# Grouped rows for the top-2 experts of the second block, an earlier softplus, and the scan's B and C rows spread by transfers

## What is computed

```python
# the scan of the first layer: B_t and C_t are 16 numbers per token, the same for all 256 channels
def step(h, t):
    delta_t, B_t, C_t, u_t = t
    dA = jnp.exp(delta_t[..., None] * A)
    h = dA * h + delta_t[..., None] * B_t[:, None, :] * u_t[..., None]
    y = jnp.einsum('bdn,bn->bd', h, C_t)
    return (h, y)
# the expert block of the second layer: E, S, H = 8, 2, 512
logits = jnp.einsum('btd,de->bte', X, Wg) + bg
topv, topi = jax.lax.top_k(logits, S)
w = jax.nn.softmax(topv, axis=-1)
xs = X[:, :, None, :] * w[..., None]
for e in range(E):
    h = jax.nn.silu(jnp.einsum('btsd,dh->btsh', xs, W1[e])) * jnp.einsum('btsd,dh->btsh', xs, W3[e])
    y = jnp.einsum('btsh,hd->btsd', h, W2[e])
    out = out + jnp.where((topi == e)[..., None], y, 0.0).sum(axis=2)
```

## Time and profile before

| | us |
|---|---|
| runs | 2838.62, 2842.82, 2860.75 (median 2842.82) |
| profiled execution, its own time | 2849.43 |
| its span, first to last instruction | 2847.6 |
| PE busy in it | 2609.8 (92%) |
| DVE busy | 1804.3 (63%) |
| ACT busy | 1235.0 (43%) |
| POOL busy | 754.6 (27%) |
| granted TensorE clock, mean | 0.929 of full |
| HBM read, written | 23.56 MB, 2.10 MB |

### The profile page before, as it was taken

The page is one execution under the profiler, slowest core; times in us unless marked ns, Lnnn a source line. Parts: engine busy times, 40 slices in busy tenths (PEclk is TensorE's granted clock), DMA queues, the critical chain, the costliest instruction groups (busy, mean ns, idle before and its releaser), DMA issues.

```text
span 2847.6 us, 35881 instructions
## 1 busy us (share of the span) xinstructions
PE 2609.8 (92%) x10560; PEld 1426.0 (50%) x10560; DVE 1804.3 (63%) x3214; ACT 1235.0 (43%) x2672; POOL 754.6 (27%) x429
## 2 busy tenths in 40 slices
PE   3267999999999999999999999999989999999999
PEld 1033555445554455545555455544555455545654
DVE  3953786567765677657866587557765587644334
ACT  2222563246532464326632466225643266323531
POOL 1311451035400353005510155003630056102200
PEclk8577899999999799998999999899999999998999
DMA  4000000000000000000000000000000000000000
GB/s 165 0 15 8 23 34 19 1 19 31 24 16 1 27 27 20 16 4 30 31 24 1 14 28 27 20 1 27 31 16 16 4 31 31 19 1 26 30 8 4
DMA packets 28590, 61.76 MB, mean 22 GB/s; under 512 B 5464, under 2 KB 5856, under 8 KB 27744
## 3 DMA queue, kind: packets, MB, share of 16 engines
q1 hardware_dynamic: 28384, 59.23, 5.8%
HBM read 23.56 MB, written 2.10 MB: 9 GB/s over the span
## 4 chain that ended last, share of the span: by engine, by line
PE 76%; issue 10%; DVE 8%; ACT 3%; POOL 2%; DMA 0%; SPq 0%; DVEq 0%; POOLq 0%; ACTq 0%
PE G L844 10%; PE G L821 9%; PE G L768 6%; PE G L769 6%; PE G L778 5%; PE G L832 5%; PE FM L821 5%; PE G L812 2%; PE G L861 2%; DVE HS L1250 2%; PE FM L748 2%; PE FM L596 2%; PE G L824 2%; PE G L568 2%; PE FM L812 1%
## 5 line engine op out<-in xcount | busy, mean ns | idle before, releaser
L1032 ACT ACTIVATE HS<-G 128x512 f32<-128x512 f32 x256 | 152.6, 596 | 608.4 <-PE G L769 607.1
L1601 POOL TENSOR_TENSOR Y<-Y,HC 128x1024 f32<-128x1024 f32 x128 | 301.1, 2352 | 351.3 <-DVE HC L1262 351.3
L844 PE MATMUL G<-REG 128*128 128x64 f32 x2560 | 383.4, 283 | 1.8
L1615 POOL TENSOR_TENSOR REG<-REG,cos_t 128x512 f32<-128x512 f32 x128 | 219.8, 1717 | 621.8 <-ACT REG L1051 621.8
L1413 DVE SCALAR_TENSOR_TENSOR HS<-HS,G 128x512 f32<-128x512 f32 x256 | 175.8, 687 | 298.7 <-ACT HS L1032 296.1
L844 PEld LDWEIGHTS G<-REG 128*128 128x128 f32 x2560 | 346.2, 201 | 11.0 <-ACT REG L1071 5.6
L1071 ACT ACTIVATE REG<-G 128x128 f32<-128x128 f32 (+3 forms) x512 | 222.2, 434 | 219.1 <-PE G L832 213.2
L1250 DVE TENSOR_TENSOR_SCAN HS<-DA,D 128x1024 f32<-128x1024 f32 x128 | 312.8, 2444 | 1.3
L821 PE MATMUL G<-REG 64*128 64x256 f32 (+3 forms) x688 | 289.8, 503 | 11.5 <-ACT REG L1063 11.3
L768 PE MATMUL G<-D,up_w 128*128 128x512 f32 x512 | 270.7, 611 | 7.8 <-DVE HC L1420 7.0
L778 PE MATMUL G<-HC,down_w 128*128 128x512 f32 x512 | 265.0, 602 | 3.9 <-DVE HC L1420 3.9
(11 more groups left out here) (249 smaller groups left out, 3947.1 us busy)
## 6 DMA issues: line engine op xcount, KB each, us to landing
REG<-ROT SPq DMA_DIRECT2D x256, 128.0 KB, 2.0
EW<-experts SPq DMA_DIRECT2D x16, 514.5 KB, 4.1
X<-xT SPq DMA_DIRECT2D x8, 256.0 KB, 3.1
W<-weights SPq DMA_DIRECT2D x1, 2048.0 KB, 9.6
up_w<-moe_up SPq DMA_DIRECT2D x1, 2048.0 KB, 15.0
gate_w<-moe_gate SPq DMA_DIRECT2D x1, 2048.0 KB, 19.1
down_w<-moe_down SPq DMA_DIRECT2D x1, 2048.0 KB, 23.4
REG<-xT SPq DMA_DIRECT2D x8, 256.0 KB, 2.6
```

Of the source, the lines that this page charges most:

```text
L844: mm = pe.matmul(G[3][:, col:col + DK], PT[:, n % 2, c * P:(c + 1) * P], V[:, c, j * P + h * DK:j * P + (h + 1) * DK], start=c == 0, stop= ...
L1601: pool.tensor_tensor(Y[:, :, :], Y[:, :, :], HC[:, n % 2, :, :], ALU.add).then_inc(y_add.sem, 1)
L1615: pool.tensor_tensor(ROT, ROT, cos_t[:, :], ALU.mult).then_inc(rope_d.sem, 1)
```

## The change

**Second expert block, by grouped rows.** Tokens are transposed to rows (`XTOK`), multiplied by their first and second pick's weight (`weigh_rows`, two POOL operations), and written to a table in DRAM, `x_rows`, sorted by expert: each expert's rows begin at a multiple of 128, so 15 tiles of 128 rows always suffice (2 x 512 rows, and at most 127 unused ones for each of 8 experts). The place of each row comes from nine bf16 matmuls on counts (`rank`) and a dozen small DVE operations (`places_of`, `number_places`). The scatter is 8 indirect transfers issued by POOL (`scatter`, in attention steps 20 to 33). The tiles come back as `XG`, are transposed on the tensor engine (`turn_rows`, 15 transposes in steps 46 to 52), and each tile is one token use: 8 up and gate matmuls and 4 down matmuls with 128 rows each instead of 512 tokens, one tanh, two DVE operations, one ACT copy, and a store to `y_rows`. The weights of a tile's expert (128 partitions x 6 KB, 786 KB) are loaded for each tile into one of three slots by SP, which reads the expert's number (`load_tile`). In the next attention phase POOL gathers each token's two results by 8 indirect transfers (`gather`, steps 1 to 14) and adds them; four transposes and one DVE add give the output, which is stored then, not at the end of `phase_1`. For the last sequence this stands in `finish`, after everything else.

**B and C by transfers.** `front_b` and `front_c` and the split into bf16 parts are gone. B and C are copied out of PSUM once (`BC`), stored to DRAM (`store_bc`), and for each state a transfer broadcasts B's and C's row to all partitions, 512 KB in SBUF, into one of two slots (`BCS`, `load_bc`). L1245 and L1262 now read their second operand from SBUF, not from PSUM.

**Softplus moved.** Its matmuls, ACT and DVE operations become starts 9, 10 and 11 of `front_start`, behind filter steps 15, 16 and 18 of `phase_1`. POOL's DU, D_skip and XNB copies also move to `phase_1`.

**Smaller.** The semaphores of a norm are merged; `M0` takes the place of `LNI`; the dense weights are no longer loaded at the start; instead `REG` is zeroed by DVE and stored once to `x_rows`, and SP waits for that before it loads the first sequence.

```diff
+MOE_ROWS = P
+MOE_TILES = (S * PICKS + EXPERTS * (MOE_ROWS - 1)) // MOE_ROWS
+SLOTS = 3
+MOE_COLS = 2 * HID + CHUNKS * D
 EXPERT_COLS = HID + CHUNKS * D + CHUNKS + 1
...
+        X_AFTER = {0: 1, 1: 2, 2: 3, 6: 4, 7: 5, 8: 6, 10: 7, 11: 8, 15: 9, 16: 10, 18: 11}
...
+        RANK_AT, PLACE_AT, NUMBER_AT, RETURN_AT = 3, 6, 19, 20
+        GATHER_AT, ADD_AT, WEIGH_AT, SCATTER_AT = (1, 4, 5, 6, 9, 12, 13, 14), 17, 15, (20, 21, 22, 25, 28, 29, 30, 33)
+        STORE_AFTER, ROWS_AFTER = 9, 11
+        TURN_AT = (46, 48, 50, 52)
...
+            def load_rows(b):
+
+                sp.wait_ge(xt_mm.sem, xt_mm.at(b - 1))
+                sp.sem_inc(sp_passed, 1)
+                sp.wait_ge(sc_in.sem, sc_in.at(b))
+                sp.sem_inc(sp_passed, 1)
+                sp.dma_start(XG[:, :, :], x_rows.rearrange("(i r) d -> r i d", r=MOE_ROWS)).then_inc(xg_in.sem, 16)
+
+            def load_tile(t, i):
+
+                k = i % SLOTS
+                if i >= SLOTS:
+
+                    sp.wait_ge(dn_mm.sem, dn_mm.at(t, i - SLOTS + 1))
+                else:
+                    sp.wait_ge(dn_mm.sem, dn_mm.at(t - 1))
+                    sp.sem_inc(sp_passed, 1)
+
+                    sp.wait_ge(place_d.sem, place_d.at(t))
+                sp.sem_inc(sp_passed, 1)
+                e = sp.value_load(tile_i[0:1, i:i + 1], min_val=0, max_val=EXPERTS - 1)
+                sp.dma_start(MW[:, k, :], moe[bass.ds(e, 1), :, :].rearrange("a p c -> (a p) c")).then_inc(mw_in[k].sem, 16)
+
+            def store_tile(t, i):
...
+            def load_bc(b, n):
+
+                if n == 0:
+                    sp.wait_ge(bc_out.sem, bc_out.at(b))
+                    sp.sem_inc(sp_passed, 1)
+                if n >= 2:
+                    sp.wait_ge(hc_mul.sem, hc_mul.at(b, n - 1))
+                else:
+                    sp.wait_ge(hc_mul.sem, hc_mul.at(b - 1))
+                sp.sem_inc(sp_passed, 1)
+                sp.dma_start(BCS[:, n % 2, :, :], bc_rows.rearrange("(k n) s -> n k s", n=STATES)[n].partition_broadcast(P)).then_inc(bc_in[n % 2].sem, 16)
...
+            def up_gate(b, i):
+
+                if i >= 2:
+
+                    pe.wait_ge(hh_d.sem, hh_d.at(b, i - 1))
+                pe.wait_ge(xt_copy.sem, xt_copy.at(b, i // TILES + 1))
+                pe.wait_ge(mw_in[i % SLOTS].sem, mw_in[i % SLOTS].at(b, i // SLOTS + 1))
+                g = 2 * (i % 2)
+                for half in range(2):
+                    for c in range(CHUNKS):
+                        at = half * HID + c * P
+                        mm = pe.matmul(G[g + half][:, c * P:(c + 1) * P], MW[:, i % SLOTS, at:at + P], XGT[:, i, :], start=True, stop=True)
+                mm.then_inc(ug_mm.sem, 1)
+
+            def down(b, i):
+                if i:
+                    pe.wait_ge(yo_copy.sem, yo_copy.at(b, i))
+                else:
+
...
+                elif p in (9, 10):
+
+                    out = bank(f"dp{p - 9}", b, f)
+                    pe.wait_ge(dt_copy.sem, dt_copy.at(f))
+                    pe.matmul(out[:, :], dt_lhs[:, (p - 9) * P:(p - 8) * P], DT, start=True, stop=True).then_inc(dp_mm.sem, 1)
 
...
 
-                    dve.wait_ge(b_mm.sem, b_mm.at(b, n + 1))
+                    dve.wait_ge(bc_in[n % 2].sem, bc_in[n % 2].at(b, n // 2 + 1))
                     if n == 0:
                         dve.wait_ge(du_d.sem, du_d.at(b))
...
                         dve.wait_ge(dn_mm.sem, dn_mm.at(b - 2))
-                    dve.tensor_tensor(HC[:, n % 2, :, :], HS[:, :, :], FC[:, :].unsqueeze(1).to_broadcast([P, HALVES, S]), ALU.mult).then_inc(hc_mul.sem, 1)
+                    dve.tensor_tensor(HC[:, n % 2, :, :], HS[:, :, :], BCS[:, n % 2, 1, :].unsqueeze(1).to_broadcast([P, HALVES, S]), ALU.mult).then_inc(hc_mul.sem, 1)
...
+            def token_use(b, i, following):
+
+                g = 2 * (i % 2)
+                dve.wait_ge(sl_act.sem, sl_act.at(b, i + 1))
+                dve.scalar_tensor_tensor(SL[:, i % 2, :], SL[:, i % 2, :], 1.0, G[g][:, :], ALU.add, ALU.mult).then_inc(sx_d.sem, 1)
+                if i >= 4:
+                    dve.wait_ge(dn_mm.sem, dn_mm.at(b, i - 3))
+                elif i == 0 and following is not None:
+
+                    dve.wait_ge(y_add.sem, y_add.at(following))
+                dve.wait_ge(sx_d.sem, sx_d.at(b, i + 1))
+                dve.scalar_tensor_tensor(HH[:, i % 4, :], SL[:, i % 2, :], 0.5, G[g + 1][:, :], ALU.mult, ALU.mult).then_inc(hh_d.sem, 1)
+
...
+            def gather(t, n):
+
+                if n == 0:
+                    for k in range(SLOTS):
+                        pool.wait_ge(yo_st[k].sem, yo_st[k].at(t))
+                    pool.wait_ge(place_d.sem, place_d.at(t))
+                    pool.wait_ge(yt_mm.sem, yt_mm.at(t - 1))
+                    pool.sem_inc(pool_passed, 1)
+                k, c = n // TILES, n % TILES
+                pool.indirect_dma_start(out=YG[:, k, c, :], out_offset=None, in_=y_rows,
+                                        in_offset=bass.IndirectOffsetOnAxis(ap=place_i[:, k, c:c + 1], axis=0)).then_inc(yg_in.sem, 16)
+
...
+            def scatter(b, n):
+
+                if n == 0:
+                    pool.wait_ge(s_rows, 17)
+                    pool.wait_ge(xw_d.sem, xw_d.at(b))
+                    pool.wait_ge(place_d.sem, place_d.at(b))
+                    pool.sem_inc(pool_passed, 1)
+                k, c = n // TILES, n % TILES
+                pool.indirect_dma_start(out=x_rows, out_offset=bass.IndirectOffsetOnAxis(ap=place_i[:, k, c:c + 1], axis=0),
+                                        in_=picked_rows[k][:, c, :], in_offset=None).then_inc(sc_in.sem, 16)
+
             def phase_1(b, t, f):
```

More of the change, by code:

```diff
@@ L435, in build, with laps @@
         block = ctx.enter_context(nc.Block())
-        def laps(eng, front, phase_1, phase_2, late=None):
+        def laps(eng, front, phase_1, phase_2, late=None, finish=None):
             front(0)
@@ L902, in phase_2 @@
                         score(b, n + AHEAD)
+                    if n == RETURN_AT:
+                        returned = take(b, ("return", 0))
+                        if t is not None:
+                            give_back(t, returned)
+                    if n in TURN_AT:
+                        g = TURN_AT.index(n)
+                        turn_rows(b, g, take(b, ("turn", g)))
                     if i == OUT_AT and j:
@@ L1648, in late, with finish @@
                 pool.wait_ge(s_late, n_late)
-            laps(pool, front, phase_1, phase_2, late)
+            def finish(t):
+                for n in range(PICKS * TILES):
+                    gather(t, n)
+                add_picks(t)
+            laps(pool, front, phase_1, phase_2, late, finish)
 def lay_out(inputs):
```

627 lines of the change are left out of this document (370 added, 257 removed).

## The result

The changed kernel takes 2950.82 us (median of 4 runs, 2944.81 to 2970.34) against 2851.78 us for the kernel before beside it (4 runs). The ratio is 1.0354 with a 95% interval of 1.027 to 1.0437: slower, where the forecast was 2718 us, a range of 2580 to 2830, and faster with a chance of 0.82. The profiled execution took 2946.96 us, its span is 2945.1 us, 97.5 more than before.

The account below looks back on a forecast made before the run. PE was taken to bound attention. From 2847.6 us, -173 -31 +3 -11 -42 +107 +3 +19 gave a span of 2722.6, and run offsets +1.8 and -6.6 gave 2718 us; range 2580 to 2830.

Parts of the forecast that it names:

- What bounds the kernel: Full laps: PE is busy 96% of the time and bounds attention, with 3.6 us of DVE slack per pair of heads.
- Expert block in phase 1: Full phase 1: grouped tiles save 44.6 us, 14 of gaps return, softplus adds 1.7; net -28.9 us a lap.
- the 1.7 us for the softplus: Phase 1: the softplus matmuls that move in cost 2 x 2 x 0.43 = 1.7 us a lap.
- The first phase 1, +3: First phase 1, with no expert block beside it: taking in the softplus adds 3 us.
- Start of phase 2: Head of phase 2: removing the softplus, against four transposes and a copy, gives -6 us a lap, -42 in all.
- B and C from SBUF: Scan products and POOL exclude each other: pairs go from 18.07 to 20.0 us, +107 over seven laps; first scan +17.
- POOL's three added operations: Phase 2: POOL's three weight and add operations cost +3 us a lap.
- B and C's transfers, hidden: Scan in phase 2: 512 KB a state lands in about 4.1 us, hidden; a swap queued behind is up to 2 us late.
- Indirect transfers, 1.2 us each, hidden: Attention steps: gathers and scatters hold POOL 1.2 us each, 19 us a lap, hidden in its free time.
- The exclusion takes everything: Rival, chance 0.10: DVE and POOL strictly alternate in phase 2, 24.1 us a pair, 2919 us; deciding mark 22.6 a pair.
- The tiles don't fill phase 1: Rival, chance 0.12: tiles delay the filter chain, phase 1 is 14 to 24 us longer than forecast; 2816 to 2886 us.
- The broadcast is slow: Rival, chance 0.03: B and C's 512 KB land after more than 9 us, each D1 waits; 2919 us.

Follow-up runs that it names:

- e9: e5 with the three softplus steps two filter steps later in phase 1 (after steps 17, 18 and 20); 2642.3 us, 0.9306 of the kernel before.
- e3: e1 with the softplus put back at the head of phase 2; 2807.4 us, 0.992 of the kernel before.
- e5: e1 with weighing on ACT, picks added by PE, two place buffers, indirect transfers in steps 4 to 7, turned rows moved, X loaded first; 2718.4 us.
- e1: The changed kernel with B and C again spread by matmul into PSUM, where the products read them; 2775.5 us, 0.9761 of the kernel before.
- e7: e1 with the B and C broadcast loads still issued from SP's queue but read by nobody; 2850.2 us, 1.0032 of the kernel before.
- e8: The changed kernel without the broadcast loads, the products reading a constant tile in SBUF; 2879.6 us, 1.013 of the kernel before.
- e2: The kernel before with only B and C moved to transfers and read from SBUF; 2976.8 us, 1.0451 of the kernel before.
- e10: e7 with the unread loads issued from ACT's queue, the later ones two attention steps later; 2802.8 us, 0.9871 of the kernel before.
- e6: The changed kernel with turned rows and returned tokens in PSUM banks FB and FC, and at other steps; 2904.9 us, 1.0224 of the kernel before.
- e11: e9 with B and C by transfers and read from SBUF again; 2873.5 us, 1.0109 of the kernel before.

## Why the prediction was wrong, by its own steps

Four steps failed: the transfers of B and C, held hidden, cost 64 to 77 us; the softplus, put at 1.7 us of matmuls a lap, cost about 10 in its place; POOL's added work and the turned rows, put at +3 a lap and at nothing but PE's time, cost 52 us; and PE's clock was carried over unchanged, so that no wait had its slow stretch behind it.

**What bounds the kernel.** Right for before, wrong as a base for the sum after it. It read PE as the bound and carried PE's clock over. With PE at 82% and not 92%, waits appear, and PE's clock (0.929 in the profiled execution before, 0.841 after) is a cost that no term had. One reading isn't among its rows: the 18 us window with DVE at 14.4 and POOL at 10.9. The trace of before gives 14.46 and 10.87 for 1360 to 1378, with PE at 17.99, so the reading holds.

**Expert block in phase 1, -28.9 a lap.** The tile's matmuls take 1.95 + 1.06 = 3.0 us at full clock, as forecast (3.1). In e9 six full phases sum to 786.2 us, 23.5 a lap less than before, with the softplus in them: PE's work falls by 39.9 (152.5 to 112.6, forecast 42.9) and the idle time grows by 16 (forecast 14). The mechanism is right, its size 5 us a lap or 32 us too large. That e9 has 131.0, the forecast's "near 131", is luck: the forecast starts from 159.5, and by the cuts used here the kernel before has 154.6, which makes it 125.7. The change itself has 137.9, and the step that failed is the 1.7 us for the softplus: it counted the matmuls and forgot that ACT's and DVE's operations are moved into a chain of dependent steps. e3 (139.0 to 128.8 in phase 1) and e9 (140.8 to 131.0) put it at 10 us a lap, 77 us in all between e5 and e9. "The first phase 1, +3" failed by the same: +8 in the change, and 101.8 us in e3, which has no softplus there, against 102.2 before; two steps later does not help in this one (108.5 in e9).

**Start of phase 2, -6 a lap.** The removal was worth it: the head is 41.5 us in e1, and 53.1 before against 42.1 after in the one lap without gathers. What the prediction did not see is what brings the head to 57 to 62 in the change. The loads, two of them right before the first swap, and the products in SBUF each have a share: the head is 47 to 54 in e7 with the loads alone and 46 to 47 in e8 with the products alone.

**B and C from SBUF, +107 and +17.** The mechanism, exclusion of whole instructions, is right, and the trace of after shows it. First scan, timeline:

```profile
77.04 1.22 DVE L1420 TENSOR_TENSOR D<-DU,BCS 128x1024 f32<-128x1024 f32 x1
...
78.29 4.31 DVE L1425 TENSOR_TENSOR_SCAN HS<-DA,D 128x1024 f32<-128x1024 f32 x1
...
77.27 3.18 POOL L1808 TENSOR_TENSOR Y<-Y,HC 128x1024 f32<-128x1024 f32 x1 [3.55 <-DVE HC L1436]
```

The first product holds POOL's Y for 0.8 us (3.18 against 2.35), and Y then holds the scan for 2.03 (4.31 against 2.28); a state takes 6.74 us where the prediction's sum gave 7.05 and 5.89 stood before. By the rule of the Trainium skill, SBUF — State Buffer, section Who interferes with whom, products with both inputs in SBUF contend with GpSimd's reads: e8 and e7 agree, 3.8 against 1.222 us at the longest. The size is near as well, 124 us forecast, 92 to 105 measured for the products by e7 and e8. That e2 has 128 for the whole part is in some measure luck, since it holds the loads too, which the 124 put at nothing. Pairs were put at 20.0, and plain ones lie at 19.2; single intervals make up for it. POOL's three added operations, put at +3 us a lap, are mis-sized: in e1, without products in SBUF, their interval is 9 us over 18.1.

**B and C's transfers, hidden.** This step failed. It priced the swap that queues behind a load at up to 2 us and let POOL's idle take it. It cost 64 to 77 us, of which 46 went when the loads left SP's queue (e10). The 4.1 us for a load was near (4.9 measured), and no wait of DVE for BCS stands in the trace of the change; what was missing is that loads stand in front of swaps, two of them at the head of each phase 2, and that a wait of PE can be followed by a stretch at half clock.

**Indirect transfers, 1.2 us each, hidden.** The price is near: the 64 gathers take 0.94 to 2.80 us, 1.235 on average, the scatters 1.6 to 1.8 on average, together 24 us of POOL a sequence where 19 were forecast. "Hidden" is wrong. Moving them, the weighing and the sum away was worth 52 us together with the new steps of the turned rows (e5 against e1). The place of the turned rows, which no step of the prediction looked at, is 37 us of the change by e6.

**The sum of the misses.** The forecast without the price of B and C is 2718 - 124 = 2594, and e9, which has everything else and good places, is at 2642. From there to the change the ratios differ by 10.5%, 298 us, along the path e9, e5, e1: 77 for the softplus, 52 for POOL's order and the turned rows, 169 for B and C. By another path the shares would be others: with everything else in place, B and C cost 228 (e11). Of the 233 us between forecast and result, some 48 lie in the size of the gain, 77 and 52 in two placements held nearly free, and 45 in B and C (169 against 124); the 11 left are the difference between ratios and medians.

**The rivals.** None of them is what happened. "The exclusion takes everything" has the side and nearly the time (2919), but its mark, 22.6 us a pair throughout, is not there: plain pairs are at 19.2. "The tiles don't fill phase 1" has a part of it, for another reason than its own. "The broadcast is slow" did not happen: loads land in 4.9 us and DVE never waits for them. Of the signs of being wrong, waits on the tiles' weights stand only in the last stretch (20.2 us of PE). The chance of 0.09 for slower came from one mechanism at a time; what came was three costs of 50 to 77 us that had been given nothing or nearly nothing, on top of the one for the products.
